# A two-layer decoder on one Trainium2 core: layer 0's cross attention and feed-forward part in one stage, and fewer states in the keys' stage

## What is computed

```python
x = LN(x + L0_attn(x))        # 16 causal heads of 16, int8-rounded k and v, LoRA
x = LN(x + L0_xattn(x, ctx))  # 16 heads of 16 over 77 keys, scores clipped at 1e4, softmax
x = LN(x + L0_ffn(x))         # act_quant, ternary w1, conv of 3 taps over time, silu, act_quant, ternary w2
x = LN(x + L1_attn(x))        # state = tanh(state * exp(A) + B x_t + b): 1024 steps, one after the other
x = LN(x + L1_xattn(x, ctx))  # 16 heads of 64 over the same context
x = LN(x + L1_ffn(x))         # layer norm, ternary w1, gelu, layer norm, ternary w2
```

## Time and profile before

| | us |
|---|---|
| median of 3 runs | 2239.9 (2236.94 to 2245.81) |
| profiled execution | 2238.17 |
| its span, first to last instruction | 2236.5 |

### The profile page before, as it was taken

How to read it: one execution, slowest core, us unless ns; L and a number is a source line. 1 busy time by engine, 2 the same in 40 slices (tenths; PEclk the granted TensorE clock), 3 DMA queues, 4 the chain that set the end, 5 groups by cost and what they waited for, 6 DMA issues and landing times. The chain is left out here.

```text
span 2236.5 us, 36076 instructions
## 1 busy us (share of the span) xinstructions
PE 1731.6 (77%) x12000; PEld 1067.2 (48%) x12000; DVE 1743.1 (78%) x4446; ACT 1374.7 (61%) x3471; POOL 887.7 (40%) x983
## 2 busy tenths in 40 slices
PE   7789999999977777776566666658399999946665
PEld 4333333333336566665445454535166666723333
DVE  4788888888636888885888888874378878769997
ACT  1116666666733343443058888889999996246665
POOL 2431000000017767763333333310286686534443
PEclk9898999999978989897777777776699999967665
DMA  2101111111020000000000000001000000000000
GB/s 73 49 12 26 30 28 28 31 31 29 12 68 15 11 32 13 13 6 20 0 13 7 1 1 1 1 1 36 24 1 20 1 1 1 1 36 17 17 19 19
DMA packets 42806, 41.53 MB, mean 19 GB/s; under 512 B 16054, under 2 KB 34670, under 8 KB 42622
## 3 DMA queue, kind: packets, MB, share of 16 engines
q1 hardware_dynamic: 42622, 39.23, 6.5%
HBM read 22.03 MB, written 4.19 MB: 12 GB/s over the span
## 5 line engine op out<-in xcount | busy, mean ns | idle before, releaser
L818 ACT ACTIVATE ST<-ST,aexp 128x1 f32<-128x1 f32 x2046 | 582.1, 385 | 2.1 <-PEq L58 2.0
L620 ACT ACTIVATE PT<-PS 128x512 f32<-128x512 f32 x576 | 309.8, 597 | 153.5 <-PE PS L371 122.5
L511 DVE CUSTOM_DVE_ANT_0 junk<-PS,maskw 128x128 bf16<-128x128 f32 (+3 forms) x512 | 226.8, 486 | 27.9 <-PE PS L348 27.9
L348 PE MATMUL PS<-KT,QT 48*128 48x512 bf16 (+3 forms) x768 | 180.5, 338 | 33.1 <-DVE MX L511 18.0
L514 DVE TENSOR_REDUCE MX<-PS 128x1 f32<-128x512 f32 x256 | 164.5, 684 | 30.0 <-PE PS L348 27.2
L392 PE MATMUL PS<-PT,VP 128*32 128x256 f32 (+1 forms) x2560 | 184.3, 370 | 0.0
L95 PE MATMUL PS<-ident,X 128*128 128x128 f32 x256 | 63.6, 338 | 135.6 <-DVE X L129 131.2
L670 POOL TENSOR_SCALAR nm<-MX 128x16 f32<-128x16 f32 x32 | 6.5, 203 | 377.8 <-DVE MX L517 377.8
L1741 PE MATMUL PS<-L_xattn_VW,l_pT 128*128 128x256 f32 (+1 forms) x640 | 143.7, 380 | 2.7 <-issue 2.7
L1725 PE MATMUL PS<-Q,l_xT 128*128 128x512 f32 (+1 forms) x384 | 144.1, 526 | 1.7 <-DVE l_s L1775 1.7
L348 PEld LDWEIGHTS PS<-KT,QT 48*128 48x128 bf16 x768 | 56.4, 93 | 183.4 <-DVE MX L511 67.9
(11 more groups left out here) (320 smaller groups left out, 4521.0 us busy)
## 6 DMA issues: line engine op xcount, KB each, us to landing
KT<-KS SPq DMA_DIRECT2D x192, 32.0 KB, 2.0
QT<-QS SPq DMA_DIRECT2D x192, 32.0 KB, 2.0
X<-in_x SPq DMA_DIRECT2D x8, 512.0 KB, 3.6
cx<-in_x SPq DMA_DIRECT2D x32, 128.0 KB, 2.0
out<-j_xn SPq DMA_DIRECT2D x32, 128.0 KB, 1.7
QT<-NMT SPq DMA_DIRECT2D x192, 2.0 KB
f_raw<-in_L_ffn_w SPq DMA_DIRECT2D x2, 1024.0 KB, 6.7
j_raw<-in_L_ffn_w SPq DMA_DIRECT2D x2, 1024.0 KB, 4.9
```

The source lines that it names most:

```text
L348: T.matmul(bank(u % 3)[:, 0:w * P], QT[i % R][rows, qt * P:(qt + 1) * P], KT[i % R][rows, k0 * P:(k0 + w) * P], start=True, stop=True).the ...
L511: V.tensor_tensor_reduce(junk[u % 3][:, 0:w * P], bank(u % 3)[:, 0:w * P], maskw[:, BANK - w * P:], 1.0, NEG, ALU.add, ALU.max, MX[i % 2][ ...
L620: C.activation(PT[n % 4][:, 2 * pr + e, 0:w], bank(3 + u % 3)[:, 0:w], ACT.Exp, scale=0.25).then_inc(e_done, 1)
L818: C.activation(self.ST[:, m, t:t + 1], self.ST[:, m, t - 1:t] if t else self.zero[:, :], ACT.Tanh, bias=self.BU[:, m, t:t + 1], scale=self ...
```

## The change

`cross_layer0` and `ffn0_and_recurrence` become one stage, `cross_and_ffn0`. Each engine's slot j runs the cross part of j while j <= LAST (now NT + 8), and from j = 20 (LAG) on, behind it, the feed-forward part of j - 20. The bodies of both parts keep their order within, but for these points:

- Waits are added where both use the same PSUM banks: the scores wait for `h`, the transposes of the quantised tile for the recurrence's inputs (R.fed, f_du), w1's and w2's products for steps of the cross part of the same slot.
- ScalarE runs 13 steps of the recurrence on each side of Silu while the cross part runs, 8 after it; 30 in the keys' stage.
- The work of `WideCross` starts when the cross part has ended (WIDE), two units a slot; it takes the context's transpose from layer 0's part, and its ring VX has five parts.
- w1 is rounded from slot 3, w2 from slot 9 with a buffer of its own, the recurrence's weights are turned from slot 5.
- Buffers share memory: `s` has three parts, not four; xb is X itself, added to behind the two rstd on GpSimd.

```diff
-        LAST = NT + 9
+        LAST, LAG = NT + 8, 20
+        WIDE, HW = LAST + 1 - LAG, P + 2
+        s, et = [in_Y1(P, SC) for _ in range(3)], [in_Y1(P, D) for _ in range(2)]
...
-        w1.host(st, ctx, 2, raw, rounded)
-        w2.host(st, ctx, 17, raw, rounded, w1)
-        R.host(st, ctx, 32)
+        R.host(st, 5, places(in_hq), places(in_y))
+        w1.host(st, ctx, 3, raw1, rounded1)
+        w2.host(st, ctx, 9, raw2, rounded2, clear=(R.turned, 4))
+        wide.host(st, places(Y2), ((d_xn, NT), (e_rsb, NT)))
...
         def sp():
...
-                if i == 16:
+                if i == 6:
                     w2.sp()
+                if i == 9:
+                    with nc.allow_non_contiguous_dma("convolution weights"):
...
+            wide.sp()
...
+        def pe_cross(j):
+            done = max(0, j - LAG)
...
+            if done >= 5:
+                T.wait_ge(R.fed, done - 4)
+                T.wait_ge(f_du, done - 4)
+            if on(e):
...
+                if done >= 1:
+                    T.wait_ge(f_h, done)
                 for at, k0, n, q, g in SCORES:
...
+                if done >= 4:
+                    T.wait_ge(qF.scaled_done, done - 3)
                 turn_weights(p, 0)
...
+        def pe_ffn(j):
+            a, c, d, other = j, j - 3, j - 4, j + LAG
+            if on(d):
+                T.wait_ge(f_hq, d + 1)
+                if d >= 1:
+                    T.wait_ge(f_hqT, d)
+                T.wait_ge(c_y, min(other, NT))
+                transposes(hq[d % 2], bank(6).bitcast(BF16), KH).then_inc(f_hqtr, 1)
+            if on(c):
+                T.wait_ge(f_silu, c + 1)
+                if c >= 1:
+                    T.wait_ge(qF.scaled_done, c)
+                T.wait_ge(d_pT1, min(other - 4, NT))
+                transposes(g[c % 2][:, :, :].rearrange("p k n -> p (k n)"), bank(4, 2), KH).then_inc(f_gtr, 1)
+            wide.pe(2 * (j - WIDE))
+            if on(d):
+                T.wait_ge(f_hqT, d + 1)
+                T.wait_ge(d_qT, min(other - 2, NT))
+                T.wait_ge(e_rsb, min(other - 8, NT))
...
+            wide.pe(2 * (j - WIDE) + 1)
...
+        def act_ffn(j):
+            b = j - 2
+            wide.act(2 * (j - WIDE))
+            if j >= 8:
+                R.act_states(13 if j + LAG <= LAST else 8)
+            if on(b):
+                C.wait_ge(f_cR, b + 1)
+                C.activation(g[b % 2][:, :, :], g[b % 2][:, :, :], ACT.Silu).then_inc(f_silu, 1)
+            wide.act(2 * (j - WIDE) + 1)
+            if j >= 8:
+                R.act_states(13 if j + LAG <= LAST else 8)
...
+        def dve():
...
+            for j in range(LAG + NT + 4):
+                if j <= LAST:
+                    dve_cross(j)
...
+                if j >= LAG:
+                    dve_ffn(j - LAG)
...
         def keys(self, act_more, bo):
...
-            act_more(90)
+            act_more(30)
```

More of the change, by code:

```diff
@@ L96, in transposes, with places, place @@
         return last
+    def places(store):
+        at = [0]
+        def place(rows, *shape, dt=F32):
+            n = int(np.prod(shape)) // (1 if dt == F32 else 2)
+            at[0] += n
+            view = store[0:rows, at[0] - n:at[0]]
+            view = view if dt == F32 else view.bitcast(dt)
+            names = "abcd"[:len(shape)]
+            return view.rearrange(f"p ({' '.join(names)}) -> p {' '.join(names)}", **dict(zip(names[1:], shape[1:])))
+        return place
     class Norm:
@@ L905, in unit, with host @@
[L905 to L913, removed]
+        def host(self, st, place, clear):
+            self.w, self.vT, self.VX = place(P, 2 * self.inner), place(P, self.nblk, B * NCTX), place(P, self.NX * self.STEP + P)
+            self.wv, self.wo, self.clear = self.w.rearrange("p (k n) -> p k n", k=2), self.w.rearrange("p (k n) -> p k n", k=8), clear
+            self.w_in, self.o_in, self.made, self.read, self.hm_step, self.zeroed, self.filled = st.sems(
+                "x_wv x_wo x_made x_read x_hm x_zeroed x_filled")
@@ L914, in unit @@
+        def unit(self, k):
+            if 0 <= k < self.nblk:
+                return "values", k
+            if self.nblk <= k < self.nblk + len(self.units):
+                return "pieces", k - self.nblk
             return None, 0
         def sp(self):
-            SP.dma_start(self.ctx_s, A["ctx_768"].rearrange("b k c -> k b c")).then_inc(self.ctx_in, 16)
+            for sem, value in self.clear:
+                SP.wait_ge(sem, value)
             for k, n in self.cw:
                 SP.dma_start(self.wv[0:n, k, :], A[self.L + "Wv"][k * P:k * P + n, :]).then_inc(self.w_in, 16)
-            SP.wait_ge(self.made, 2 + self.nblk)
+            SP.wait_ge(self.made, self.nblk)
@@ L926, in dve_heads, with pe @@
                     V.memset(self.hm[64 * h:64 * h + 64, e:e + 1], float(e == h)).then_inc(self.hm_step, 1)
-        def pe(self, j):
-            kind, n = self.unit(j)
+        def pe(self, k):
+            kind, n = self.unit(k)
             if kind is None:
                 return
[L932 to L937, removed]
-                    last = T.transpose(bank(7)[0:m, b * NCTX:(b + 1) * NCTX], self.ctx_s[:, b, k * P:k * P + m], ident[0:NCTX, 0:NCTX])
-            elif kind == "values":
+            if k >= 1:
+                T.wait_ge(self.read, k)
+            if kind == "values":
                 T.wait_ge(self.w_in, 32)
-                for k, m in self.cw:
-                    last = T.matmul(bank(7)[:, 0:B * NCTX], self.wv[0:m, k, n * P:(n + 1) * P], self.ctxT[0:m, k, :], start=k == 0, stop=k == 1)
+                for c, m in self.cw:
+                    last = T.matmul(bank(7)[:, 0:B * NCTX], self.wv[0:m, c, n * P:(n + 1) * P], self.ctxT[0:m, c, :], start=c == 0, stop=c == 1)
             else:
@@ L1661, in ffn0_and_recurrence @@
+            for j in range(LAG + NT + 4):
+                if j <= LAST:
+                    pool_cross(j)
+                if j >= LAG:
+                    pool_ffn(j - LAG)
         sp()
```

847 lines of the change are left out of this document (404 added, 443 removed).

## The result

The changed kernel takes **2256.0 us** (median of 5 runs, 2254.1 to 2260.5), against 2242.3 for the kernel before on the same chip: a ratio of **1.007, with a 95% interval of 1.0054 to 1.0086**. It is slower. The forecast was 10 us faster, so the sign is wrong, although the range (2200 to 2261) holds the time. One of the five runs of e1 took 4901.7 us and is left out of its ratio.

The account below looks back on a forecast made before the run. VectorE was taken as the engine with least room, ScalarE's chain as the bound of slots 28 to 35. Merge -1, slots 41 to 55 -8, states -1: -10 from 2239.9 gives 2230 us, range 2200 to 2261.

Parts of the forecast that it names:

- Part 5: Slots 36 to 40: cross attention drains (20.5, 17.3), then ScalarE's work gives 16.6 us in three slots; sum 88 us.
- Part 6: Slots 41 to 55, feed-forward alone: TensorE's clock stays at its upper level and L1560's 1.33 us wait goes; -8 us.
- Part 3: Slots 20 to 27: filling takes 62 us, then four full merged slots of 25.0 us set by VectorE, 100 us.
- Part 4: Slots 28 to 35, recurrence beside both parts: ScalarE's chain with two table loads sets 26.4 us a slot, 211 in all.
- Part 1: Keys' stage, 90 steps to 30: worth 0 to -0.5 us there; fourteen steps more elsewhere, -1 us in cross attention 1.
- Part 2: Slots 0 to 19, cross attention alone: w2's six conversions move here, 6 us; VectorE's clip of slot 20 at 855.
- Two separate slots cost 24.7: A cross slot of 11.03 and a feed-forward slot of 13.7 us, so a full merged slot of 25.0 wins nothing.
- Rival 3: Each table switch holds ScalarE about 1.4 us longer than its load: +22, 2252 us; chance 0.07.
- or a unit comes late: Slots 41 to 55: if the values' unit comes late or the clock level doesn't stay up, 0 to +6 us.
- The slower one: Chain through ScalarE with TensorE at the lower clock in the cross part: 27 us more, 2257 us; chance 0.17.

Follow-up runs that it names:

- e1: Changed kernel with the recurrence's states spread as before (9 and 9 a slot, 90 in the keys' stage): 2252.0 us, ratio 1.005 to the kernel before.
- e2: Changed kernel with GpSimd's middle tap moved to the slot's start and its bias addition between division and subtraction: 2256.4 us, ratio 1.0078.
- e5: Changed kernel with both e1's spread of states and e2's order on GpSimd: 2235.6 us, ratio 0.9985.
- e3: Changed kernel with Tanh in the place of layer 0's Silu, so that no table loads alternate: 2255.9 us, ratio 1.0069.
- e7: e5 with 12 states ahead of Silu and 3 behind in slots 36 to 39, none in the last two slots, 138 in the keys' stage: 2261.6 us.
- e10: Changed kernel with 90 states in the keys' stage and none in the first four slots of cross attention 1: 2239.4 us, ratio 1.0005.
- e4: e1 with LAG = 41, so that the feed-forward part starts when the cross part has ended: 2241.8 us, ratio 1.0014.

## Why the prediction was wrong, point by point

In the sum, two terms failed. Part 5 mis-sized slots 36 to 40, the last three of them reckoned from ScalarE's work alone (88 us, measured 100.1), and Part 6 counted on the upper clock level (-8 us, measured +6.6). Together they miss by 26.7 of the 31 us. In the mechanism, the step that failed is in Parts 3 and 4: VectorE's work of the two stages was added up with no term for GpSimd, whose additions hold the taps for 2.5 us a slot. That miss was hidden in the number, by the luck that ScalarE's chain had been put at nearly the same length.

**Part 1** was right on the keys' stage: it stayed as long, and ScalarE sat idle in two thirds of it (36.1 us). It was wrong on what follows: 14 tokens more were to be worth 1 us and were worth nothing, since the slots of cross attention 1 are the same to 0.1 us in both traces. The forecast read ScalarE's 132.0 of 134.1 us as a stage bound by ScalarE throughout. The stretch in fact began with 30 us in which nothing but states ran. Reading that stretch in its timeline would have shown it.

**Part 2** and the filling slots came out at +2.9 us over the 917, and that is luck. Slot 20 began near 850.3 and not at 855: the slots ahead of it took 1.5 us more than before, not 6. Slots 20 to 23 then took 69.6 us and not 62. The first groups of taps are held there too (6.41 and 4.91 us in slots 22 and 23), but e2, with 4.09 and 2.18, took no less from slot 20's clip to slot 24 (64.3 us for 63.5), so what these 7.6 us are stays open.

**Part 3**, the full merged slot. Forecast 25.0, measured 26.2 in slots 24 to 27 (104.6 for 100). The step that failed is the adding up itself: it took 13.65 us for the feed-forward part's work on VectorE over into a slot in which GpSimd works on other things at other times. In the later slots of the kernel before, GpSimd's middle tap and bias addition lay beside VectorE's waits and operations that read PSUM; in the merged slot they stand behind the cross part's operations on GpSimd and so fall on the taps, for 2.5 us. Without that the slot is 23.9 (e2, e5), 1.1 better than forecast; the copy's wait, 1.6 us and not 2.3, is 0.7 of it. "Two separate slots cost 24.7" was right, and so merging would win 0.8 us a slot.

**Part 4**, 26.4 for ScalarE's chain, measured 25.8 on average (26.3 falling to 24.7). The number is nearly right and the cause is not: e1 and e3 took 4.5 and 2.6 us a slot off ScalarE, and slots 28 to 35 together gave 1.6 us (e1) and nothing (e3). It would have come true only without the held taps; then ScalarE's loop does decide (27.2 in e2). The table loads were forecast right in their length of 1.28 us (there are 30 and not 28: the kernel before has 4, to which 26 come). Rival 3 is out: in the slot shown an activation starts 0.01 to 0.02 us after its load, the load 0.01 to 0.03 us after the instruction ahead of it, and taking 28 of them out changed nothing (e3). The drain of 1.38 us in the Trainium skill (page ScalarE: Activation LUTs, section "What ACT_TABLE_LOAD costs") doesn't show here.

**Part 5** was mis-sized by 12 us. Its slots took 24.7, 20.8, 18.1, 18.4 and 18.1 us for 20.5, 17.3 and three times 16.6. The last three were reckoned from ScalarE's work alone. They are a chain: X's update, transposes, ScalarE's copies behind 26 half-steps, hidden transposes at the lower level, with the held L169. Of the 18.2 us, 1.3 hang on the states (e1); the remaining 17 did not follow them in e7. What would bring them to 13.7 was not found. The miss of 7.7 us in the first two slots was not split; in e5, with fewer states and free taps, they take 24.8 and 17.8 us, so the first one's 4 us is due to neither.

**Part 6**, -8 us expected and +6.6 measured (204.6 for 198). The level didn't rise (granted clock 0.75 from 1335 to 1376 us): with 2.98 us of idle time left ahead of X's transposes instead of 4.20, four matmuls of L1435 still took 2.08 and the wait of 1.33 stayed, so the slots took 13.7. This is the row in one of the later slots:

```profile
1449.51 0.44 PE L95 MATMUL PS<-ident,X 128*128 128x128 f32 x2 [2.98 <-DVE X L142]
...
1452.08 2.08 PE L1435 MATMUL PS<-DwT,U 128*128 128x256 f32 x4
```

Four slots around 50 took 13.9 to 15.0 us, 2.9 more in all: the unit ahead of w2's product had grown to 1.90 us (1.51), and the transposes ahead of it took 1.92 at the lower level. The text had named that ("or a unit comes late"). And 2.3 us are ScalarE's backlog at the stage's end, a step that the sum didn't have. The last 1.4 us were not placed, and no run raised the level to show what it would give.

**The rivals.** The slower one named ScalarE at the lower clock level and 2257 us. The time nearly agrees, but not the mechanism: its slots were to be over 28 us. Nothing in the list was a clash of GpSimd with VectorE, although the prediction itself quotes such a case (normalisations of 0.81 for 0.40 us beside GpSimd) and even took it off as a gain of merging. The trace of the kernel before holds the very case, in the third slot of its feed-forward stage, where GpSimd comes late and its two operations (1061.54 to 1065.42) fall on the taps:

```profile
1061.62 5.53 DVE L1571 SCALAR_TENSOR_TENSOR f_g<-f_h,f_cw,f_c 128x128 f32<-128x128 f32 x8 [0.68 <-POOL f_c L1656]
```

That is 5.53 us where the group takes 2.18, and this line's longest tap is 2.05 us there as well. So the price could have been read before the change was made.

## What to carry to other kernels

When work moves in time, ask of each operation not only what it waits for but what runs beside it on the engine that it gets in the way of: list VectorE's operations that take their tensors from SBUF, those with two inputs first, and lay GpSimd's new times over them. A line whose longest instruction is six times its median may be such a clash. When two loops are of almost equal length, taking time off one shows nothing, and each suspected cost must be removed together with the other before it is called free. And look at a stage's first and last slots for filler work such as these states: what is free in the middle stands alone there, and TensorE stood idle for 20.9 us at the entry of the next stage both before and after the change. Freeing it was worth 17 us in the merged kernel (e10).

## What was not expected of the hardware

A tap of 0.34 us that meets a GpSimd operation lasts until that one's end (1.18 and 2.05 us). So do operations from SBUF to SBUF that read one tensor: L169 took 1.23 us for 0.35 (changed kernel), L142 2.10 for 0.40 (e2). A copy and a reduction out of PSUM beside the same addition took their usual 0.69 and 1.23 us (e4). A table load in front of an activation cost 1.28 us of ScalarE and no more, and nothing at all in time where ScalarE had slack (e3).
